# Expert results written to one row per token and choice, and summed on TensorE at the end, in place of additions in DRAM

## What is computed

```
def _moe(x, rw, rb, w1, b1, w2, b2):
    ...
    router_weights = jax.nn.softmax(xf @ rw + rb, axis=-1)
    topw, topi = jax.lax.top_k(router_weights, K)
    topw = jax.nn.softmax(topw, axis=-1)
    combine = jnp.zeros((T, E), xf.dtype).at[jnp.arange(T)[:, None], topi].add(topw)
    h = jax.nn.gelu(jnp.einsum('td,edf->etf', xf, w1) + b1[:, None, :], approximate=False)
    eo = jnp.einsum('etf,efd->etd', h, w2) + b2[:, None, :]
    out = jnp.einsum('etd,te->td', eo, combine)
...
x = _layernorm(x + _moe(x, router_w, router_b, e_w1, e_b1, e_w2, e_b2), ln3_g, ln3_b)
```

## Time and profile before

| | us |
|---|---|
| median of 3 executions | 807.43 (806.61 to 808.73) |
| the profiled execution, its time | 807.22 |
| the profiled execution, span of the core | 805.4 |
| PE busy in the span | 720.3 |
| DVE, ACT, POOL busy | 404.0, 376.5, 260.7 |

### The profile page before, as it was taken

One profiled execution on the slowest core, in us unless ns is written; L12 is line 12 of the kernel. 1 busy time (PEld: TensorE's weight loads), 2 busy tenths in 40 slices (PEclk: granted clock), 3 DMA queues, 4 the chain that ended last, 5 costly groups with the idle time before them and its releaser, 6 DMA issues.

```text
span 805.4 us, 14606 instructions
## 1 busy us (share of the span) xinstructions
PE 720.3 (89%) x5227; PEld 496.8 (62%) x5227; DVE 404.0 (50%) x972; ACT 376.5 (47%) x774; POOL 260.7 (32%) x434
## 2 busy tenths in 40 slices
PE   6789999999999999999987799997699999999920
PEld 4534434455556554645653577886699999999920
DVE  5588777757767777655686454364011011100135
ACT  3224556566566676667743345322333333333313
POOL 8140300423243412422642244311423333333225
PEclk9899999999999999999998899999799999999975
DMA  8960340452047103214228735788589999999843
GB/s 263 304 170 14 118 121 4 118 161 82 1 118 202 22 6 85 85 38 131 52 71 303 228 126 155 239 256 282 178 253 337 333 316 326 326 341 325 257 121 108
DMA packets 98656, 140.42 MB, mean 174 GB/s; under 512 B 11775, under 2 KB 85733, under 8 KB 96101
## 3 DMA queue, kind: packets, MB, share of 16 engines
q1 hardware_dynamic: 78581, 110.08, 42.9%
q10 hardware_dynamic: 12896, 19.92, 7.5%
q0 software_dynamic: 7104, 9.45, 5.9%
HBM read 108.55 MB, written 30.88 MB: 173 GB/s over the span
## 4 chain that ended last, share of the span: by engine, by line
PE 54%; DMA 29%; DVE 5%; issue 5%; ACT 2%; POOL 2%; ACTq 1%; SPq 1%; POOLq 0%; DVEq 0%
DMA sums_scratch<-arena,scatter_rows 22%; PE out_acc L952 10%; PE score_pair L929 8%; PE work L899 8%; PE work L873 5%; PE work L816 4%; DMA arena<-parts_scratch 4%; PE work L822 3%; PE work L976 3%; PE work L885 2%; DVE neg_part_max L1426 2%; PE score_pair L932 2%; PE work L960 2%; PE work L902 2%; DMA parts_scratch<-arena_more 1%
## 5 line engine op out<-in xcount | busy, mean ns | idle before, releaser
L1426 DVE TENSOR_REDUCE neg_part_max<-work 128x1 f32<-128x512 f32 (+4 forms) x368 | 213.7, 626 | 89.6 <-PE work L899 44.3
L1196 ACT ACTIVATE arena<-score_pair 128x1024 f32<-128x1024 f32 (+2 forms) x224 | 178.6, 839 | 92.4 <-PE score_pair L932 61.1
L899 PE MATMUL work<-arena 96*128 96x77 bf16 (+4 forms) x640 | 122.3, 284 | 15.7 <-DMA arena<-parts_scratch 8.2
L929 PE MATMUL score_pair<-arena 99*128 99x512 bf16 (+2 forms) x448 | 113.0, 335 | 2.8 <-DMA arena<-negmax_scratch 1.4
L1836 POOL DMA_INDIRECT sums_scratch<-arena,scatter_rows x36 | 56.7, 1574 | 179.4 <-DMA sums_scratch<-arena,scatter_rows 127.4
L952 PE MATMUL out_acc<-arena 128*32 128x512 f32 (+4 forms) x896 | 104.2, 517 | 4.8 <-ACT arena L1196 4.4
L899 PEld LDWEIGHTS work<-arena 96*128 96x128 bf16 x640 | 49.7, 101 | 79.3 <-issue 42.7
L822 PE MATMUL score_pair<-arena 128*128 128x256 f32 x432 | 97.5, 379 | 0.0
L1356 DVE TENSOR_TENSOR arena<-score_pair,arena 128x256 f32<-128x256 f32 x27 | 11.5, 425 | 170.6 <-PE score_pair L822 161.1
L816 PE MATMUL work<-arena 128*128 128x128 f32 x720 | 89.8, 285 | 0.7 <-ACT arena L1129 0.5
L816 PEld LDWEIGHTS work<-arena 128*128 128x128 f32 x720 | 87.3, 201 | 1.4 <-ACT arena L1129 0.6
(11 more groups left out here) (244 smaller groups left out, 889.4 us busy)
## 6 DMA issues: line engine op xcount, KB each, us to landing
arena<-in_L_xattn_e_w SPq DMA_DIRECT2D x54, 1024.0 KB, 7.7
arena<-parts_scratch SPq DMA_DIRECT2D x24, 768.0 KB, 6.9
arena<-in_L_xattn_e_w ACTq DMA_DIRECT2D x18, 1024.0 KB, 5.8
parts_scratch<-arena_more SPq DMA_DIRECT2D x24, 384.0 KB, 3.3
parts_scratch<-arena_more SPq DMA_DIRECT2D x24, 256.0 KB, 3.4
parts_scratch<-arena_more SPq DMA_DIRECT2D x24, 128.0 KB, 3.6
residual<-in_x SPq DMA_DIRECT2D x4, 512.0 KB, 8.0
tokens_scratch<-residual SPq DMA_DIRECT2D x2, 1024.0 KB, 6.1
```

Of the source, the lines that this page charges most:

```text
L899: m = pe.matmul(bank[:, j * it.w:(j + 1) * it.w], qa[st.half(it.g)][0:R_S, h, n0:n0 + P], k, start=True, stop=not it.last)
L929: m = pe.matmul(st2[pair][0:rows, j, 0:w], k, qa[st.half(it.g)][0:R_M, h, skip:QG], start=True, stop=not diagonal)
L1196: act_e.activation(pt[buf][0:rows, :, 0:w], st2[pair][0:rows, :, 0:w], ACT.Exp, scale=float(HD) ** -0.5).then_inc(pair_taken[pair], 1)
L1426: dve.tensor_reduce(pm[:, it.at, it.t, it.h0:it.h0 + it.nh], bank[:, 0:it.nh * it.w].rearrange("p (j k) -> p j k", j=it.nh), AX.X, ALU.max ...
```

## The change

`sums_scratch` (a row per token) is replaced by `chosen_scratch`, with 4096 rows, one for each token and choice, and 128 more for empty slots. The list `scatter_rows` now holds choice x 2048 + token, and `gather_rows` is made from it by masking the upper bit (one more small DVE instruction in each `lists`). `put(j)` takes the place of `add_up(j)`: a plain indirect write, without the wait for the write before it. `keep` no longer writes the token rows to a second array, and the zeros for it are gone. The third of three multiplications that place the slot weights moves from POOL (L1947) to DVE (L1724, now three times). PE's block of slot weights stands one tile later.

The loads of tiles 9, 10 and 11 are put into `ORDER` ("A3"), directly behind `lists` and ahead of the last three `t_put`.

At the end SP loads both choices of each piece into a new tile `chosen` (16 DMAs of 256 KB in place of 8). PE sums: 8 matmuls of 512 columns with the identity as weights copy the tokens, still in `residual`, into 8 PSUM banks, and then two more for each piece add the two choices in the same bank. DVE reads each piece from PSUM. PE begins when every `up_taken` and `y_taken` is complete, which includes the branches of tiles 36 to 38.

```diff
-        steps += [Item("t_down", t=j - 1), Item("t_add", t=j - 1)] * (j > 0)
-    return steps + [Item("t_down", t=NFIRST - 1), Item("t_add", t=NFIRST - 1)]
+        steps += [Item("t_down", t=j - 1), Item("t_put", t=j - 1)] * (j > 0)
+    return steps + [Item("t_down", t=NFIRST - 1), Item("t_put", t=NFIRST - 1)]
...
-    "RZLRLRNL2CUNHPKSTZU2YU2EOIXY2Z2DZW"
+    "RZLRLRNL2CUNHPKSTZU2YU2EOIA3XY2Z2DZW"
...
-        sums_d = nc.dram_tensor("sums_scratch", [T + P, D], f32, kind="Internal").ap()
+        chosen_d = nc.dram_tensor("chosen_scratch", [2 * T + P, D], f32, kind="Internal").ap()
...
+        chosen = arena[:, self_only:self_only + 2 * NT * D].rearrange("p (c t n) -> p c t n", c=2, t=NT)
...
-                if j == NFIRST:
+                if j == NFIRST + 1:
                     e.wait_ge(weights_v, 2)
-                    e.wait_ge(weights_g, 1)
                     i, use = invert_at
                     find_slots(bank_of(invert_at), weight_j, NT).then_inc(up_full[i], 1)
+                if j == NFIRST:
+                    pass
                 elif j <= NSURE:
                     down(j - 1)
...
+            for i in range(6):
+                e.wait_ge(up_taken[i], (uses[0] + 5 - i) // 6)
+            for j in (NSLOT - 2, NSLOT - 1):
+                e.wait_ge(y_taken[j % 2], y_use(j))
...
+            for n in range(NT // PIECE):
+                pe.matmul(sum_bank(n), ident[:, :], piece(res, n), start=True, stop=False)
+            for n in range(NT // PIECE):
+                e.wait_ge(*sums_in(n))
+                for c in range(2):
+                    m = pe.matmul(sum_bank(n), ident[:, :], piece(chosen[:, c], n), start=False, stop=(c == 1))
+                m.then_inc(summed, 1)
...
-                dve.tensor_copy(rows_in[:, NFIRST:], ids).then_inc(rows_ok, 1)
+                own.inc(dve.tensor_copy(rows_out[:, NFIRST:], ids))
+                e.wait_ge(vstep, own.n)
+                dve.tensor_scalar(rows_in[:, NFIRST:], rows_out[:, NFIRST:], T - 1, None, ALU.bitwise_and).then_inc(rows_ok, 1)
...
-                        for i in range(2):
+                        for i in range(KINDS):
...
-                e.wait_ge(*sums_in(n))
+                e.wait_ge(summed, n + 1)
                 for t in tiles:
-                    own.inc(dve.bn_stats(stat[:, t % 2, :], res[:, t, :]))
+                    own.inc(dve.bn_stats(stat[:, t % 2, :], sum_of(t)))
...
-                    m = dve.scalar_tensor_tensor(res[:, t, :], res[:, t, :], mv[:, t, 0:1], param[:, G3, :],
+                    m = dve.scalar_tensor_tensor(res[:, t, :], sum_of(t), mv[:, t, 0:1], param[:, G3, :],
...
-            def add_up(j):
+            def put(j):
                 pool.wait_ge(y_ok, j + 1)
-                if j:
-                    pool.wait_ge(*slot_y_out(j - 1))
                 pool.indirect_dma_start(
-                    sums_d[0:S] if j < NFIRST else sums_d, bass.IndirectOffsetOnAxis(ap=rows_out[:, j:j + 1], axis=0), slot_y[j % RINGY], None,
-                    compute_op=ALU.add).then_inc(slot_y_out(j)[0], 16)
+                    chosen_d, bass.IndirectOffsetOnAxis(ap=rows_out[:, j:j + 1], axis=0), slot_y[j % RINGY], None).then_inc(
+                    slot_y_out(j)[0], 16)
...
-            e.wait_ge(rows_ok, 2)
-            e.wait_ge(tokens_out[1], 2 * 16)
-            load(NFIRST)
-            for j in range(NFIRST + 1, NFIRST + RINGX - 1):
-                load(j)
-            e.wait_ge(kinds_ok, 2)
-            pool.tensor_tensor(weight_j[:, :, 2, :], row_j[:, :, 0, :], by_n(kinds[:, 3, :]),
-                               ALU.mult).then_inc(weights_g, 1)
...
-                    for to in (tokens_d, sums_d):
-                        sp.dma_start(to[it.b * S:(it.b + 1) * S, :].rearrange("(t p) n -> p t n", p=P),
-                                     res[:, it.b * TB:(it.b + 1) * TB, :]).then_inc(tokens_out[it.b], 16)
+                    sp.dma_start(tokens_d[it.b * S:(it.b + 1) * S, :].rearrange("(t p) n -> p t n", p=P),
+                                 res[:, it.b * TB:(it.b + 1) * TB, :]).then_inc(tokens_out[it.b], 16)
...
             for n in range(NT // PIECE):
-                sp.dma_start(res[:, n * PIECE:(n + 1) * PIECE, :], rows_of(sums_d, n * PIECE)).then_inc(sums_in(n)[0], 16)
+                for c in range(2):
+                    sp.dma_start(chosen[:, c, n * PIECE:(n + 1) * PIECE, :], rows_of(chosen_d[c * T:(c + 1) * T], n * PIECE)).then_inc(
+                        sums_in(n)[0], 16)
```

57 lines of the change are left out of this document (29 added, 28 removed), and 2 rows, old and new, of the table KINDS_OF_WORK.

## The result

The changed kernel takes 795.14 us, median of 6 executions (790.34 to 802.18), beside 806.70 for the kernel before (805.62 to 808.73): a ratio of 0.9862, 95% interval 0.9813 to 0.9910. The forecast was 800.2, with a range of 796.6 to 803.4. So the sign is right, and the gain was larger than the range allowed. Two more measurements of the same kernel, on two other occasions, gave 796.58 (ratio 0.9888, 0.9856 to 0.9920) and 796.56 (0.9879, 0.9848 to 0.9910). The mean of the three ratios is 0.9876, which on the 807.43 of before is 797.4.

What follows compares the result with a forecast made beforehand. It took PE to bound tiles 9 to 35, with losses where PE or its path waits for POOL. Seam -10.7 and end +3.5 gave -7.2 us on 807.22, 800.0, forecast 800.2 against the median; range 796.6 to 803.4.

Steps and rivals of the forecast that it cites:

- What bounds the kernel: Tiles 9 to 35: PE is fully busy and additions merely keep step; what counts is where PE waits for POOL.
- The seam, -10.7: Between down(7) and up(9): loads no longer wait for additions, up(9) starts at 561.2 instead of 571.94, saving 10.7 us.
- the rival of late gathers: At the seam: gathers queue like the weights, up(9) starts at 564.2, 3 us less gain, 803.2; chance 0.10.
- no gather of 36 took over 6.6: At the seam: the argument given against gathers landing late, from landing times before the change.
- The clock at the seam: At up(9): PE's clock still falls, loss of 1.6 us as before; on the edge, 1.6 us more gain in the range.
- a kind clock: Clock stays up at the seam, at the token matmuls' start, or both: 796.9 to 798.6; chance 0.14.
- The end, +3.5: Behind the last result: PE's token copying comes last, DVE starts at 783.9 instead of 780.40, 3.5 us lost.
- inside 3.3 to 4.36: At the end: bounds in us from the last plain write's issue to the first load's issue.
- DVE's pace, unchanged by PSUM: At the end: DVE still takes 1.94 us a piece reading PSUM; the rival of dearer reads had chance 0.09.
- The missing waits of POOL in the string save nothing: In the string: no gain, since PE waits at no other load for more than 0.3 us.
- The dropped second copy of the tokens and the zeros were off the path.: Ahead of the seam: dropping these transfers was counted as no gain.
- The range: Whole kernel, 796.6 to 803.4: meant to take in the kind clock, late gathers and dearer PSUM reads.

Runs made afterwards that it cites:

- e1_seam_alone: Kernel before with loads of tiles 9 to 11 ahead of the last three additions, third multiplication on DVE, slot weight block one tile later; ratio 0.9936.
- f1_after_again: The changed kernel, unaltered, measured again on another occasion; 796.56 us, ratio 0.9879 to the kernel before.
- e5: Kernel before with the seam's part of the change and the load of tile 12 also ahead of the last three additions; ratio 0.9899.
- e7: Kernel before with the seam's part, loads of tiles 9 to 12 ahead, second sequence's second copy behind the weights of tile 10; ratio 0.9883.
- e4_own_bank: The changed kernel with PE's token matmuls waiting only for their own banks, DVE's marks needed for pieces 6 and 7 alone; ratio 0.9876.
- e9_chained_writes: The changed kernel with each plain write again waiting until the write before it has landed; ratio 0.9883.
- f3_before_late_copy: Kernel before, additions and stalled seam kept, with the second array's copy of the second sequence written some 45 us later; 802.51 us, ratio 0.9955.
- e2_end_alone: The changed kernel with its three loads put back behind the last three writes, undoing the seam's part; 805.14 us, ratio 0.9995.
- e8_both_queues: The changed kernel, token matmuls waiting only for their own banks, ACT issuing second-choice loads of the first four pieces; ratio 0.9874.

## Why the prediction was right and wrong

- **What bounds the kernel** (POOL's additions keep step with PE, so nothing is gained by faster ones for tiles 9 to 35): true of the stall as it stood, 198.38 against 198.54. It doesn't hold once the seam is shorter. With additions 4 of the 10.9 us are given back. The forecast's -10.7 for the seam is right because the change takes both steps at once. For the order of loads alone the same reasoning is 4 us too high, and the expectation of e1_seam_alone was.
- **The seam, -10.7**: measured -10.9, with the steps in the order told. The gathers were in before ACT was ready, so the rival of late gathers failed. The argument against it was weaker than it read: over the kernel gathers took up to 7.2 us to land, median 6.2, against 6.6 and 4.4 before, so "no gather of 36 took over 6.6" was no bound.
- **The clock at the seam**, taken as before: right for after (the first 32 instructions took 2.87 + 2.44 = 5.3 us, before 3.40 + 1.79 = 5.2), but f1_after_again ran up(9) at the full clock and its stretch is 1.6 us shorter. It is on the edge, as the text said. Of the eleven profiled executions with the shortened seam the clock fell in eight and stayed up in three (f1, e5, e7), where the prediction gave a kind clock, at either place, 0.14.
- **The end, +3.5**: measured +3.3 to the end of the span and 13.57 - 10.08 = +3.5 to DVE's first piece. The first load came 3.97 us behind the last write, inside 3.3 to 4.36. The token matmuls come last by some 2.3 us, for the first piece alone: with them out of the way, in e4_own_bank, the second piece waits for its loads. The size also hangs on the clock, and e9_chained_writes lost 1.2 us more by it.
- **DVE's pace, unchanged by PSUM**: 1.92 to 1.95 us for a piece against 1.94. By form, after's statistics and two-input instructions from PSUM answer to the earlier trace rows:

```profile
L1812 DVE SCALAR_TENSOR_TENSOR residual<-work,mean_var,param_rows 128x256 f32<-128x256 f32 x6 | 2.6, 479 | 0.1
L1806 DVE BATCH_NORM_STATS2 stat<-work 128x6 f32<-128x256 f32 x6 | 2.2, 416 | 12.0 <-PE work L1132 12.0
```

479 ns from PSUM stand against 495 from SBUF for the two-input form, and 416 from PSUM against 406 from SBUF (L1780 of before) for the statistics. So the rule of the Trainium skill ("VectorE: DVE Perf Modes", the section on TRN2 errata), by which PSUM's larger fixed part would cost 2.1 us, does not show here. The trace decides for no cost: 10 ns more for one form and 16 less for the other.
- **The missing waits of POOL in the string save nothing**: right ahead of down(7). f3_before_late_copy keeps them all and shows the step without them. In e2_end_alone they gave 2.15 us at the seam, which in the changed kernel is part of the 10.9.
- **The step that failed: "The dropped second copy of the tokens and the zeros were off the path."** Nobody waits for that copy, and so I costed it at nothing, with no row behind it. Beside the matmuls of tiles 6 and 7 it makes ACT's read of the expert number 0.6 us longer, and mostly PE's clock falls just behind that wait: 2.2 us in the trace of before, and 3.6 us in f3_before_late_copy's ratio. The seven profiled executions with plain writes and one copy show a step of -1.6 us on average (-0.6 to -2.2). With that the forecast is 800.2 - 1.6 = 798.6, with the 2.2 it is 798.0, with the ratio 796.6; the three measurements, on 807.43, are 796.3 to 798.4, mean 797.4. The price is shown on the kernel before. On the changed kernel, where the copy was put back, the time doesn't settle it. For the zeros and for the first sequence's copy no price is shown: up to 527 us the traces of kernels with the zeros lie 2.5 us ahead of before to 4.5 behind, those without them 4.3 ahead to 3.8 behind.
- **The range**: 796.6 to 803.4 took in costs that hardly came and ended near the best case of the named terms. It had no term for the stretch ahead of down(7), in which two executions of one kernel differ by up to 9 us; medians of six came out between 795.1 and 796.6. That the first ratio lies below the range and the other two inside it is no more than this scatter. What is left between the corrected sums and the mean, about 1 us either way, is within the intervals and I can't assign it.

## What to carry to other kernels

A DMA that nobody waits for is not free: look at what it overlaps, and whether an engine there is one short gap away from a lower clock; here moving it 45 us later was worth 3.6 us. When two steps of a change touch one queue, measure each alone, since the order of loads kept its 10.9 us only with plain writes. When a profile books a delay as issue, look at the small register reads in front of it. And cut a trace at fixed instructions and compare stages: stages here repeat to some tenths where the clock is the same, whole executions to 9 us.

## What the runs showed of the hardware

- A plain scattered write of 128 rows costs POOL 0.98 us of issue against 1.57 for an addition, and the queue's packets fall from 7104 to 3648 in the kernel. Its time to landing is hardly shorter: 2.4, 6.3, 7.6 us (least, median, most) in after against 3.7, 6.4, 8.2 in before. I had expected some 4 us for a chained write; in e9_chained_writes the median was 6.1.
- A fall of the clock to 0.50 at a short gap cost 1.6 us in the next 32 instructions of an up (5.47 against 3.84 us) and 1.7 in the first sums (7.01 against 5.31 us in e8_both_queues, behind a wait of 2.2). It fell at the seam in after and not in f1_after_again, with the same gap of 3 us in the same place.
- A register read by ACT (TENSOR_LOAD of the expert number) took 0.27 or 0.28 us at one place in nine traces, and 0.88 to 0.97 in the five in which a second copy of 1 MB from SBUF to DRAM was under way.
- Issuing loads from two queues let 256 KB take 3.6 to 8.2 us to land in place of 2.8 to 7.1: more in flight, no sooner there.
